# Output bias of an attention block kept in f32: added by VectorE while it reads the projection, gate applied by GpSimd, eleven rooms of probabilities in place of twelve

## The reference

```python
xn = _layernorm(x, axis=-1)
# attention: q, k, v = xn W^T + b; scores / sqrt(32), masked by (i % 256) >= (j % 256); softmax
out = attn.transpose(0, 2, 1, 3).reshape(B, L, D)
s = jnp.einsum('bld,ed->ble', out, Wo) + bo            # the output bias
y = jnp.einsum('bsi,oi->bso', xn, where(weights >= 0, 1, -1)) * scale + bias
g = _silu(jnp.clip(y, -100, 100))
return x + s * g
```

## Time and profile before

| | us |
|---|---|
| median of 3 runs (1747.96 to 1748.9) | 1748.41 |
| the profiled execution | 1749.87 |
| its span in the profile | 1748.0 |
| PE busy | 1682.2 (96%) |
| DVE busy | 1320.4 (76%) |
| ACT busy | 1220.3 (70%) |
| POOL busy | 1160.3 (66%) |

### The profile page before, as it was taken

One profiled execution on the slowest core, in us unless ns is written; L12 is line 12 of the kernel. 1 busy time (PEld: TensorE's weight loads), 2 busy tenths in 40 slices (PEclk: granted clock), 3 DMA queues, 4 the chain that ended last, 5 costly groups with the idle time before them and its releaser, 6 DMA issues.

```text
span 1748.0 us, 34003 instructions
## 1 busy us (share of the span) xinstructions
PE 1682.2 (96%) x11652; PEld 777.4 (44%) x11652; DVE 1320.4 (76%) x2620; ACT 1220.3 (70%) x2854; POOL 1160.3 (66%) x1154
## 2 busy tenths in 40 slices
PE   8999999999999999999999999999999999999978
PEld 3443444444444444444444444444444444444323
DVE  6888678787678777787777867788677886688772
ACT  4587776776667766678766777657776677676774
POOL 0067666775867667775578855688656776767763
PEclk9999999999999999999999999999999999999989
DMA  7314311343124322243122431224212342122111
GB/s 202 114 38 86 73 44 50 98 91 75 37 62 106 92 50 56 64 104 84 38 74 62 109 78 29 74 74 104 68 44 56 92 86 60 34 62 73 44 50 49
DMA packets 185038, 126.09 MB, mean 72 GB/s; under 512 B 106912, under 2 KB 159264, under 8 KB 184416
## 3 DMA queue, kind: packets, MB, share of 16 engines
q1 hardware_dynamic: 183904, 123.13, 28.0%
q10 hardware_dynamic: 960, 0.79, 0.2%
HBM read 41.50 MB, written 17.05 MB: 33 GB/s over the span
## 4 chain that ended last, share of the span: by engine, by line
PE 76%; ACT 16%; DVE 4%; issue 3%; POOL 1%; ACTq 0%; DMA 0%; SPq 0%; DVEq 0%; POOLq 0%
PE pJ L488 26%; PE pO L692 14%; PE pS L649 10%; PE pT L673 9%; ACT pS L808 6%; PE pT L669 3%; PE pJ L580 3%; ACT PT L796 3%; PE pJ L581 3%; PE pJ L584 3%; PE pS L652 2%; ACT acc L796 2%; DVE mx L1008 1%; PE pT L633 1%; ACT xs L719 1%
## 5 line engine op out<-in xcount | busy, mean ns | idle before, releaser
L1008 DVE TENSOR_REDUCE mx<-pS 128x1 f32<-128x512 f32 (+3 forms) x1216 | 780.2, 656 | 292.3 <-PE pS L649 190.7
L796 ACT ACTIVATE PT<-pT 128x512 f32<-128x512 f32 (+1 forms) x1092 | 637.5, 594 | 413.1 <-PE pT L673 366.9
L1177 POOL TENSOR_TENSOR acc<-acc,PT 128x512 f32<-128x512 f32 x620 | 756.5, 1256 | 37.8 <-PE pO L692 37.8
L673 PE MATMUL pT<-QK 97*128 97x512 f16 (+3 forms) x1280 | 393.0, 318 | 17.6 <-ACT acc L796 10.9
L649 PE MATMUL pS<-QK 96*128 96x512 f16 (+3 forms) x1280 | 391.9, 319 | 16.5 <-ACT pS L808 10.5
L808 ACT ACTIVATE pS<-pS,a 128x384 f32<-128x384 f32 (+3 forms) x512 | 277.0, 547 | 8.3 <-DVE a L1023 8.0
L692 PE MATMUL pO<-PT,V 128*32 128x512 f32 (+3 forms) x2824 | 265.1, 487 | 0.6
L488 PE MATMUL pJ<-xT,wh_q 128*128 128x512 f16 x512 | 192.6, 381 | 1.9 <-ACT xT L737 1.5
L669 PE MATMUL pT<-QK 128*128 128x128 f16 x1024 | 180.9, 220 | 13.1 <-ACT PT L796 10.1
L488 PE MATMUL pJ<-wh_v,xT 128*128 128x512 f16 x512 | 192.1, 378 | 0.8 <-ACT V L776 0.8
L649 PEld LDWEIGHTS pS<-QK 96*128 96x128 f16 x1280 | 124.1, 97 | 154.4 <-ACT pS L808 35.4
(11 more groups left out here) (161 smaller groups left out, 2342.7 us busy)
## 6 DMA issues: line engine op xcount, KB each, us to landing
QK<-sg SPq DMA_DIRECT2D x756, 64.0 KB
xs<-in_x SPq DMA_DIRECT2D x60, 256.0 KB, 3.1
xr<-in_x SPq DMA_DIRECT2D x58, 256.0 KB, 3.1
out<-xr SPq DMA_DIRECT2D x58, 256.0 KB, 2.5
QK<-aT SPq DMA_DIRECT2D x256, 1.0 KB, 1.7
rq<-moved SPq DMA_DIRECT2D x132, 2.0 KB, 1.7
QK<-in_x SPq DMA_DIRECT2D x8, 256.0 KB, 4.4
QK<-in_mqk SPq DMA_DIRECT2D x2, 512.0 KB, 10.1
```

Source lines behind the costliest of these rows:

```text
L673: ins = e.matmul(slot[:, to:to + 512 - q0], k4[0:97, j, kc], q4[0:97, j, q0:512], start=True, stop=True)
L796: e.activation(probabilities_at(i), t_bank("t", i)[:, 0:cols], ACT.Exp, scale=SS).then_inc(s_p, 1)
L1008: e.tensor_reduce(mx[:, par, part, :].rearrange("p (j q) -> p j q", q=4)[:, heads[0]:heads[-1] + 1, qi], s_bank("s", i)[:, 0:cols].rearran ...
L1177: e.tensor_tensor(a, a, PT[:, RING_AT[i] % NPT, 0:width * len(heads)].rearrange("p (j q) -> p j q", j=len(heads)), ALU.add).then_inc(s_ap, 1)
```

## The change

The bias no longer goes through PE.

- The combined bias is made for all 128 partitions (`bvc` filled in every column, `bo` loaded by broadcast), kept in f32 and halved: `brow` is now 128x512 f32. DVE makes it with two instructions, before with three.
- The 64 products with `brow` are gone; the first product of the projection now starts the bank.
- For tiles 0 to 59 DVE computes `tt = 0.5 SS pJ + brow` as it takes the bank, no longer waiting for the gate (`s_u`) but for POOL's end of the tile before (`s_f`), since there is one `tt`. POOL multiplies `tt` by the gate, then adds x.
- For tiles 60 to 63 a new strand on POOL, `last_bias`, computes gate times bias and adds it to x beforehand, in two instructions per tile, so the end of the kernel keeps its form.
- The memory for the wider `brow` and for `tt` comes from the ring: `NPT` is 11.
- Due times are changed in many places. In each batch the result products of the fourth and the seventh tile change places with a qk projection, and other pieces move by less.

```diff
-NPT = 12
+NPT = 11
@@ wish
-        return 4 * SL * a + (-97.65, -93.55, -92.31, -87.5, -63.31, -75.95, -58.02, -57.58)[b]
+        return 4 * SL * a + (-97.65, -94.47, -92.31, -87.5, -64.95, -75.95, -58.02, -58.04)[b]
...
-        return 4 * SL * (a + 1) + (-8.68, -1.88, 8.27, 20.34, 36.36, 39.53, 41.48, 58.21)[b]
+        return 4 * SL * (a + 1) + (-8.22, -1.88, 8.27, 22.63, 36.36, 39.53, 43.83, 56.8)[b]
@@ build
-        brow = sb("brow", [P, D], F16)
+        brow = sb("brow", [P, D], F32)
+        tt = sb("tt", [P, D], F32)
@@ tensor: project_o (and project_last alike)
-                        ln.wait_ge(s_br, 3)
+                        ln.wait_ge(s_br, 2)
-                        e.matmul(out, row32[:, :], brow[:, :], start=True, stop=False)
                         for g in range(NG):
...
-                            e.matmul(out, Onh[:, n, ts], Wh["o"][:, g, :], start=False, stop=False)
+                            e.matmul(out, Onh[:, n, ts], Wh["o"][:, g, :], start=g == 0, stop=False)
@@ vector: output_bias
-                e.tensor_tensor(Y[:, :], bank("b", 0)[:, :], bob[:, :], ALU.add).then_inc(s_br, 1)
+                e.tensor_tensor(brow[:, :], bank("b", 0)[:, :], bob[:, :], ALU.add).then_inc(s_br, 1)
                 ln.wait_ge(s_br, 1)
-                e.tensor_scalar(brow[:, :], Y[:, :], SW, None, ALU.mult).then_inc(s_br, 1)
-                ln.wait_ge(s_br, 2)
-                e.scalar_tensor_tensor(brow[32:64, :], Y[32:64, :], SW, brow[32:64, :], ALU.mult,
-                                       ALU.subtract).then_inc(s_br, 1)
+                e.tensor_scalar(brow[:, :], brow[:, :], 0.5, None, ALU.mult).then_inc(s_br, 1)
@@ vector: results
-                    ln.wait_ge(s_u, i + 1)
+                    ln.wait_ge(s_br, 2)
                     ln.wait_ge(s_op, i + 1)
-                    e.scalar_tensor_tensor(gate(i), bank("o", b, t)[:, :], 0.5 * SS, gate(i), ALU.mult, ALU.mult).then_inc(s_t1, 1)
+                    if i < NTILE - NLAST:
+                        ln.wait_ge(s_f, i)
+                        e.scalar_tensor_tensor(tt[:, :], bank("o", b, t)[:, :], 0.5 * SS, brow[:, :], ALU.mult, ALU.add).then_inc(s_t1, 1)
+                    else:
+                        ln.wait_ge(s_u, i + 1)
+                        ln.wait_ge(s_rb, 2 * (i - NTILE + NLAST + 1))
+                        e.scalar_tensor_tensor(gate(i), bank("o", b, t)[:, :], 0.5 * SS, gate(i), ALU.mult, ALU.mult).then_inc(s_t1, 1)
@@ gpsimd: results
+                    value = gate(i)
+                    if i < NTILE - NLAST:
+                        value = tt[:, :]
+                        ln.wait_ge(s_u, i + 1)
+                        e.tensor_tensor(value, value, gate(i), ALU.mult).then_inc(s_tg, 1)
+                        ln.wait_ge(s_tg, i + 1)
...
-                    e.tensor_tensor(result(i), gate(i), rest(i), ALU.add).then_inc(s_f, 1)
+                    e.tensor_tensor(result(i), value, rest(i), ALU.add).then_inc(s_f, 1)
@@ gpsimd: new
+            def last_bias():
+                for k in range(NLAST):
+                    i = NTILE - NLAST + k
+                    yield max(at_gate(i, 4) + 0.8, at_t(T_FIRST[NU - 2, 0]) + 6)
+                    part = HL[0][:, :, :].rearrange("p a d -> p (a d)").bitcast(F32)
...
+                    e.tensor_tensor(part, gate(i), brow[:, :], ALU.mult).then_inc(s_rb, 1)
...
+                    e.tensor_tensor(rest(i), rest(i), part, ALU.add).then_inc(s_rb, 1)
```

More of the change, by code:

```diff
@@ L225, in at_ln @@
         first = x0 + (-50.92 if b == 1 else -88.73)
-        return first, first + 4.56, 0.59, first + 15.16
+        return first, first + 4.56, 0.59, first + 15.65
     return x0 + -14.94, x0 + -15.33, 0.49, x0 + -5.64
@@ L1209, in results @@
                         ln.wait_ge(s_rest, 16 * NT)
-                    e.tensor_tensor(result(i), gate(i), rest(i), ALU.add).then_inc(s_f, 1)
-            in_time(additions(), first_layer_norm(), layer_norm(), normalise(), gates(), results())
+                    e.tensor_tensor(result(i), value, rest(i), ALU.add).then_inc(s_f, 1)
[4 more added lines that the diff above has]
+                    part = HL[0][:, :, :].rearrange("p a d -> p (a d)").bitcast(F32)
+                    ln.wait_ge(s_u, i + 1)
+                    ln.wait_ge(s_br, 2)
+                    ln.wait_ge(s_xd[0], 16 * (NTILE - NT) // 2)
+                    ln.wait_ge(s_rb, 2 * k)
+                    e.tensor_tensor(part, gate(i), brow[:, :], ALU.mult).then_inc(s_rb, 1)
+                    ln.wait_ge(s_rest, 16 * NT)
+                    ln.wait_ge(s_rb, 2 * k + 1)
+                    e.tensor_tensor(rest(i), rest(i), part, ALU.add).then_inc(s_rb, 1)
+            in_time(additions(), first_layer_norm(), layer_norm(), normalise(), gates(), results(), last_bias())
         @block.sync
```

62 lines of the change are left out of this document (31 added, 31 removed).

## The result

The changed kernel takes 1752.15 us (median of 20 runs), the kernel before, on the same chip, 1749.41 (20 runs). The ratio is 1.0015, with a 95% interval from 1.0008 to 1.0022: 2.7 us slower, little, but clear of the noise of these runs. A second set of runs gave 1751.86 against 1749.77, 1.0012 [1.0003, 1.0020]. One execution of experiment 15 ran in a slower state (1778.67 us at a granted clock of 0.94) and is left out. The forecast was 1737.9, its range 1731 to 1746. So 14.2 us that were forecast are missing, 1.0 of them because the kernel before has 1749.41 over 20 runs and not the 1748.41 from which the forecast was made.

A forecast was written before the change was run, and what follows sets the result against it. PE was taken to set the pace from 100 to 794 us, ACT and DVE at 794 to 815, ACT from 1640 to 1710. 1749.87 - 13.8 + 2.8 + 0.5 = 1739.4, or 1737.9 against the median; range 1731 to 1746.

The forecast's parts named there:

- What POOL pays: POOL's 68 new instructions, 10.2 us per batch: hidden but for one place per batch, 0.4 each, 2.8 us in all.
- the end: After 1698.73 us: six new POOL instructions end 1.3 us too late for scaling `On`; cost between 0 and 1.3, taken 0.5.
- What goes: 64 bias products leave PE, on the path where PE is full, 0.215 us each: 13.8 us gained.
- the late place: 794 to 815 us, each batch: POOL's additions after the Newton iteration end 0.9 later; DVE, then PE's row sums, wait.
- the bounds of 0 and 0.9: Cost per batch at 794 to 815: 0 if DVE's and ACT's new order absorbs the delay, 0.9 if all reaches PE.
- What DVE pays: DVE's bank-taking instruction stays at 679 ns and its new wait for POOL has 0.95 us of room: nothing counted.
- the second engines pay more: Rival, 8%: the whole 0.9 per batch and as much again through DVE's lengthened instructions at 794 to 815: 1747.7 us.
- the 32 us more on DVE: If each of 68 new POOL instructions cost DVE 0.47 us: 32 us, 4.1 per batch, hidden except where DVE is late.
- The rival that POOL becomes the late engine: Rival, 7%: the odd unit's last additions end later, up to 3.2 us per batch; the kernel gets slower, 1757.8 us.
- Eleven rooms: PT ring one shorter: ACT waits 0.4 us for POOL's eighteenth addition near 800 us, once per batch; seven batches, 2.8.
- The retimed order: Rival, 15%: layer norm moved forward closes PE's old gaps at 794 to 815, one us per batch back: 1728 us.

The follow-up runs named there:

- experiment 15: Changed kernel with last_bias spread, earlier gate addition and waiting multiplication, ACT's layer norm 1.64 later, three additions given to DVE: 1742.04 us (five executions).
- experiment 5: Changed kernel without POOL's 60 multiplications, the gate left out of those tiles: 1741.32 us, 0.9953 of the kernel before.
- experiment 2: Kernel before with one more POOL multiplication ahead of each of the first 60 results (wrong factor in the result): 1770.47 us, 1.0123.
- experiment 1: Kernel before with its 64 bias products left out, so the output bias is missing: 1737.98 us, 0.9937.
- experiment 14: Changed kernel with last_bias spread, earlier gate addition and waiting multiplication, and ACT's layer norm of each batch's second half 1.64 later: 1739.27 us, 0.9940.
- experiment 13: Changed kernel with the three 384-wide additions behind POOL's Newton iteration given to DVE, once per batch: 1754.78 us, 1.0035.
- experiment 10: Changed kernel with last_bias spread: one pair of instructions stays, three go further back on POOL: 1746.15 us, 0.9982 of the kernel before.
- experiment 8: Changed kernel with POOL's addition and clamp of one gate per batch (sixth tile) one addition earlier: 1751.79 us, 1.0011 of the kernel before.
- experiment 3: Kernel before with eleven rooms for PT in place of twelve: 1750.28 us, 1.0006.
- experiment 4: Changed kernel with all due times and lengths of the kernel before put back: 1763.51 us, 1.0085 of the kernel before.
- experiment 16: The changed kernel run again, nothing changed: 1751.86 us, 1.0012 of the kernel before.
- experiment 7: Changed kernel with layer norm of each batch's second half back by 1.6 us on DVE, POOL and ACT: 1751.77 us, 1.0013 of the kernel before.
- 12: Changed kernel with last_bias spread, the sixth gate's addition earlier and the fifth tile's multiplication waiting for DVE's row shift: 1738.99 us, 0.9942 of the kernel before.

## Why the prediction was wrong

The step that failed is in **What POOL pays**: "I looked for the places where something waits for POOL. There is one in each batch." I looked at waits that were there, and put the whole term at 2.8 us for that one place. Taking the multiplications out gives 10.8 (experiment 5). They cost where no wait was: put into the kernel before, 1.61 a batch at 701 to 754 and 0.80 at 857 to 912, against 0.06 at the place I had worked out (experiment 2); in the changed kernel, 0.98 at 701 to 754. Before the change POOL is idle for 10.6 us in the stretch from 701 to 754, but for only 0.5 of the 22 us ahead of 747, where its addition for the gate is needed in time. With the second step, the end (0.5 forecast, 4.9 measured), this is what is missing.

Point by point:

- *What goes, 13.8.* Right: PE's work fell by 13.7. As a change of its own it is worth 11.3 (experiment 1), so some 2 us of it are lost again without any new work on POOL.
- *POOL, 0.4 a batch at the late place.* From 754 to 805 the changed kernel loses 1.25 a batch, outside the bounds of 0 and 0.9; with the stretch behind it, which gets better, 0.66, and without the falls of the clock 0.3. That the last lies near 0.4 is luck: it is not made of the term that I had. In the old order the multiplications are hidden there. POOL's busy time rose by 92.9 us, where 68 x 1.27 is 86; line 1215 takes 1374 ns on average. The mechanism (DVE waits longer than 2.41, PE longer than 0.45) is there: DVE waits 2.80, and PE 0.87 once ACT is out of the way (experiment 14). In the changed kernel ACT's own order comes first, which I had not seen: layer norm stands ahead of the tile. But taking either wait away gains nothing (experiments 13 and 14).
- *What DVE pays, nothing.* `tt` takes 677 ns on average, as taken. Its new wait for POOL, more than a few tenths of which I had named as a sign of being wrong, is 8.5 us in all, in three of the last four of these instructions; experiment 10 has it too and gains, so it is not what costs. But I had counted only the instruction that takes the bank. Its lateness, 0.8 us near 746 through `Y`, the tanh and the gate, is a price of POOL's multiplication that reaches PE by way of DVE.
- *The rival "the second engines pay more", 8%.* This was the true kind, priced at 1747.7 and at the wrong place. I let DVE's lengthened instructions count only at the late place, and I took them from line 1113. The ones that matter are the small ones that turn row maxima into shifts, for which ACT and PE wait: they make the price of experiments 2 and 8. In the changed kernel itself the holding at 746 is no longer than before (0.88 on `a<-mx`, before 1.03 on `mx<-mx`); its price there is the lateness through `Y`. Of the 32 us more on DVE nothing came: it is busy for 1321.1 us, 1320.4 before, and line 1112 takes 1043 ns on average, 1153 before. (68 x 0.47 us is 4.0 per batch, not 4.1; nothing hangs on it.)
- *The rival that POOL becomes the late engine, 7%.* Its place was the last additions of the odd unit and its price 1757.8. The kernel did get slower, and DVE does wait longer there, but giving these additions to DVE gains nothing (experiment 13); this was not the way.
- *Eleven rooms.* No cost by themselves in the old order (experiment 3), as the bound of 0 allowed. In the new order, for which the 0.4 was worked out, no run tests them.
- *The end, 0.5.* The term is mis-sized: it measured 4.9. The six instructions take 8.8 us and not 7.62, DVE's `R` is ready 1.2 earlier than before, and the cover that I named, PE's reader of `Onl`, is not the first to be reached: `Onh` is ahead of `PT` tiles on ACT. Experiment 10 gives back 6.0 us.
- *The retimed order.* The new times are worth 11.4 us against the load (experiment 4), not 9.8 beyond the forecast as the first rival had it.

The sum of what was forecast and what was not: -13.7 of work, +6.9 at 701 to 754, +4.0 at 754 to 857, -1.6 at 857 to 912, +4.9 at the end and 1.3 scattered make +1.8, and the profiled spans differ by 1.7 (1749.7 and 1748.0).

## What to carry to other kernels

Before work is moved to POOL, ask not only who waits for POOL now. Ask first whether POOL has idle time just ahead of each result that must be on time; its average over a batch (60 us here) does not tell. Then ask which short DVE instructions on the way to PE lie beside the new ones: one of 0.17 us took 1.2 beside a long POOL instruction here, and a wait of 0.38 on POOL saved it. An instruction that is held and for which nobody waits costs nothing, so compare what PE loses and not the lengths. And look at what stands behind a late instruction on the next engine: at the end, PE stood for tiles that ACT had behind `Onh`, not for `Onh`.

## What the runs showed of the hardware

**Short DVE instructions are held until a POOL instruction ends, by shape.** The groups of `a<-mx` and `mx<-mx` by form, kernel before and then changed (count, busy us, mean ns, idle us):

```profile
L1023 DVE TENSOR_SCALAR a<-mx 128x4 f16<-128x4 f32 x32 | 4.8, 150 | 0.3
L1023 DVE TENSOR_SCALAR a<-mx 128x2 f16<-128x2 f32 x64 | 16.1, 251 | 1.5
L1023 DVE TENSOR_SCALAR a<-mx 128x1 f16<-128x1 f32 x256 | 38.1, 149 | 5.6
L1047 DVE TENSOR_SCALAR a<-mx 128x16 f16<-128x16 f32 x31 | 5.4, 175 | 1.1
L1043 DVE TENSOR_TENSOR mx<-mx 128x16 f32<-128x16 f32 x31 | 17.1, 551 | 0.0
```

```profile
L1022 DVE TENSOR_SCALAR a<-mx 128x4 f16<-128x4 f32 x32 | 9.5, 297 | 4.2
L1022 DVE TENSOR_SCALAR a<-mx 128x2 f16<-128x2 f32 x64 | 20.5, 320 | 1.5
L1022 DVE TENSOR_SCALAR a<-mx 128x1 f16<-128x1 f32 x256 | 36.9, 144 | 4.7
L1046 DVE TENSOR_SCALAR a<-mx 128x16 f16<-128x16 f32 x31 | 11.1, 360 | 1.3 <-DVE mx L1042 0.3
L1042 DVE TENSOR_TENSOR mx<-mx 128x16 f32<-128x16 f32 x31 | 6.0, 193 | 0.8
```

The forms of `a<-mx` with 16, 4 and 2 columns got longer, by 14.8 us in all. The 256 with one column did not, and neither did any row maximum (1216 of them, the longest 694 ns in either kernel) nor the taking of a bank (693 ns at most), which have an operand in PSUM. `mx<-mx`, with both inputs in SBUF, was held before (551 ns on average) and is so less now, by 11.1 us. So in sum the holding grew by 3.7 us only; what it costs depends on who waits. The Trainium skill, "SBUF — State Buffer", section "Who interferes with whom", says that a `tensor_scalar` on SBUF can enter a mode that uses both of DVE's ports, that DVE and GpSimd then shut each other out for a whole instruction, the one that issues first going first, and that `tensor_reduce` on this chip never takes part. The traces agree: in experiment 2 DVE's instruction, begun 0.11 us after POOL's of 1.26, took 1.19. The prediction had weighed only the sentence beside it, on two inputs in SBUF.

**The granted clock fell in some batches and not in others, after the same wait.** PE waits 1.65 us for ACT's tile near 803 and again near 1013. Two executions of the changed kernel, the first and the one of experiment 16 (columns as above, the granted clock is the third from the end):

```profile
803.00:823.00 20.00, 18.03 (x127) 7.24 (x128) 14.15 (x33) 19.02 (x48) 6.31 (x6) 1.00 0.36 80
1013.00:1033.00 20.00, 18.81 (x124) 7.04 (x122) 13.53 (x32) 18.53 (x45) 6.08 (x6) 0.91 0.45 80
```

```profile
803.00:823.00 20.00, 18.67 (x121) 7.41 (x118) 12.92 (x30) 17.90 (x46) 7.13 (x6) 0.91 0.45 80
1013.00:1033.00 20.00, 18.26 (x126) 7.22 (x119) 14.00 (x33) 18.49 (x45) 7.34 (x7) 1.00 0.47 80
```

1.00 is the upper level, 2.4 GHz, for the whole stretch; 0.91 means that part of it ran at the lower one, 1.2 GHz. The same program has it at 1013 once and at 803 the other time, so the fall is not tied to a place in the code. Nor is it tied to the wait of 1.65: in experiment 7, whose longest wait of PE there is 0.95, the clock is at 0.91 from 594 to 614 and from 1013 to 1033, and at 1.00 from 803 to 823; in experiments 14 and 15, with waits up to 0.97 and 1.48, it is at 1.00 in all three. What decides it stays open. A batch with it is longer by 0.8 us (210.28 and 210.15 between first results, where 209.50 and 209.37 stand without). Over the 20 executions of the result the changed kernel's mean granted clock lay between 0.986 and 0.990, with the longest times at the lowest clock; the kernel before, beside the experiments, had 0.991 to 0.995. In the kernel before, whose longest wait there is 0.85, both stretches are at 1.00. So the falls are a part of what is missing. How much they cost beyond the 0.8 of a batch is not shown; experiment 14, with none in its batches and 0.992 to 0.995, is no faster than 12, with 0.989 to 0.993.
